# Four homes for the experts' weights, bank pairs by kind in a first pass, and values cast on two engines in turn

## The reference, cut to what matters

```python
x = x + xattn0(layernorm(x), ctx)      # 16 heads of 16, softmax over 12544 keys, then a small MLP
x = x + attn0(layernorm(x))            # causal, 16 heads of 16
x = x + experts0(layernorm(x))         # top 2 of 8: gelu(x @ W1[e] + b1[e]) @ W2[e] + b2[e], W1 256 x 1024
x = x + xattn1(layernorm(x), ctx)      # 16 heads of 64, softmax over 12544 keys
x = x + attn1(layernorm(x))
x = x + experts1(layernorm(x))         # top 2 of 8, silu gated
# xattn: q = x @ Wq; k = ctx @ Wk; v = ctx @ Wv; softmax(q k^T * scale) v @ Wo
```

## Time and profile before

| | before |
|---|---|
| median of 3 runs | 1709.82 us (1706.11 to 1713.38) |
| profiled execution | 1709.02 us, span 1707.3 us |
| TensorE busy | 1469.4 us, 86% |
| VectorE busy | 1085.0 us, 64% |
| ScalarE busy | 1095.1 us, 64% |
| granted TensorE clock, mean | 0.959 of full speed |

### The profile page before, as it was taken

One profiled execution on the slowest core, in us unless ns is written; L12 is line 12 of the kernel. 1 busy time (PEld: TensorE's weight loads), 2 busy tenths in 40 slices (PEclk: granted clock), 3 DMA queues, 4 the chain that ended last, 5 costly groups with the idle time before them and its releaser, 6 DMA issues.

```text
span 1707.3 us, 37451 instructions
## 1 busy us (share of the span) xinstructions
PE 1469.4 (86%) x15312; PEld 989.3 (58%) x15312; DVE 1085.0 (64%) x1663; ACT 1095.1 (64%) x1612; POOL 91.0 (5%) x90
## 2 busy tenths in 40 slices
PE   4777776999997698978898976999999899999959
PEld 2333334777775486434444434777777677777748
DVE  4687775111112303667777778888888888888842
ACT  4998985777773134756766664767677676776721
POOL 5211110000000003100000000000000000000000
PEclk8999998999998699999999997999999999999979
DMA  3232216434332055554444434777777577788530
GB/s 125 84 113 76 88 64 176 88 67 90 76 67 99 0 198 176 167 179 151 149 149 149 151 141 96 138 136 135 138 136 136 107 137 136 137 219 163 143 111 4
DMA packets 122415, 209.00 MB, mean 122 GB/s; under 512 B 8236, under 2 KB 113158, under 8 KB 122246
## 3 DMA queue, kind: packets, MB, share of 16 engines
q1 hardware_dynamic: 122246, 206.60, 47.5%
HBM read 142.22 MB, written 64.36 MB: 121 GB/s over the span
## 4 chain that ended last, share of the span: by engine, by line
PE 45%; DVE 21%; ACT 16%; issue 15%; DMA 3%; SPq 0%; DVEq 0%; POOL 0%; ACTq 0%; POOLq 0%
PE ps L590 44%; ACT ps L966 7%; DVE W L1140 6%; DVE v L1140 4%; DVE v L1252 4%; DVE small L1204 3%; ACT p L1003 2%; ACT p L991 2%; ACT W L989 1%; DMA W<-in_L_ffn_W_dram 1%; ACT W L991 1%; DMA keys_hi<-p 1%; DVE W L1170 1%; ACT stage L976 1%; ACT p L966 1%
## 5 line engine op out<-in xcount | busy, mean ns | idle before, releaser
L966 ACT ACTIVATE p<-ps 128x512 f16<-128x512 f32 (+1 forms) x490 | 327.7, 679 | 195.6 <-PE ps L590 193.0
L1140 DVE TENSOR_TENSOR p<-ps,p 128x512 f16<-128x512 f32 (+1 forms) x467 | 351.5, 753 | 127.8 <-ACT p L991 65.6
L590 PE MATMUL ps<-W,q_all 128*32 128x128 f32 (+2 forms) x2268 | 220.2, 303 | 58.2 <-DVE W L1170 33.1
L590 PEld LDWEIGHTS ps<-q_all,W 128*128 128x128 f16 (+1 forms) x3544 | 232.6, 99 | 57.2 <-issue 6.7
L590 PE MATMUL ps<-q_all,W 128*128 128x128 f16 (+2 forms) x3544 | 263.1, 227 | 0.9 <-DVE q_all L1136 0.7
L966 ACT ACTIVATE ps<-ps 128x512 f32<-128x512 f32 x392 | 233.7, 596 | 0.0
L590 PEld LDWEIGHTS ps<-W,q_all 128*32 128x32 f32 (+2 forms) x2268 | 110.1, 110 | 152.3 <-DVE W L1170 44.9
L590 PE MATMUL ps<-wv,ctxT_a_hi 128*128 128x512 f16 (+1 forms) x588 | 157.6, 350 | 33.0 <-DVE v L1140 32.7
L590 PE MATMUL ps<-v,p 128*128 128x130 f16 x3136 | 169.7, 207 | 5.1 <-DVE p L1140 5.1
L1243 DVE COPY q_all<-ps 128x256 f32<-128x256 f32 x98 | 37.0, 420 | 206.4 <-PE ps L590 206.3
L1003 ACT CAST p<-ps 128x896 f16<-128x896 f32 x180 | 151.0, 934 | 14.1 <-PE ps L590 13.8
(11 more groups left out here) (218 smaller groups left out, 1710.0 us busy)
## 6 DMA issues: line engine op xcount, KB each, us to landing
W<-keys_hi SPq DMA_DIRECT2D x56, 896.0 KB, 14.4
W<-keys_low SPq DMA_DIRECT2D x28, 896.0 KB, 11.4
keys_hi<-p SPq DMA_DIRECT2D x75, 224.0 KB, 1.9
keys_low<-p SPq DMA_DIRECT2D x75, 224.0 KB, 1.9
keys_hi<-W SPq DMA_DIRECT2D x65, 224.0 KB, 1.9
keys_low<-W SPq DMA_DIRECT2D x65, 224.0 KB, 1.9
W<-in_L_ffn_W_dram SPq DMA_DIRECT2D x10, 1024.0 KB, 8.4
W<-in_ctx_dram SPq DMA_DIRECT2D x14, 672.0 KB, 4.4
```

The source lines that it names most:

```text
L590: return pe.matmul(out_, lhsT, rhs, start=start, stop=stop, **kw)
L966: return act.activation(out_, in_, ACT.Exp, scale=scale)
L1140: return dve.tensor_tensor(out_, a, b, op)
```

## The change

Three things change.

Experts: `EXPERT0` gives each expert two half homes, and there are four whole ones; the fourth is made of a part of `W` and of `p16`, which attention 0 uses up to its last tile. Every expert has its own load semaphore. Expert 3 is asked for once attention 0 has weighed its last tile, 4 after one down product, 5 after two, 6 after four, 7 after five. Wq and Wk follow expert 7, Wv and Wo the last down product.

First pass: a function `pairs_of` gives each turn its pair and the turn that last used it. For the first attention that is the same as before. For the second, keys turns alternate between pairs 0 and 1 and max turns between pairs 2 and 3.

Tile loop: for odd tiles ScalarE casts the values ahead of its exponentials, and VectorE only subtracts.

```diff
+        def pairs_of(turns, apart):
+            pairs, before, count, last = [], [], {"keys": 0, "max": 0}, {}
+            for i, (kind, n, h) in enumerate(turns):
+                if apart:
+                    pair = count[kind] % 2 + (0 if kind == "keys" else 2)
+                    count[kind] += 1
+                else:
+                    pair = i % 4
+                pairs.append(pair)
+                before.append(last.get(pair))
+                last[pair] = i
+            return pairs, before
+
+        (PAIR0, BEFORE0), (PAIR1, BEFORE1) = pairs_of(TURNS[0], False), pairs_of(TURNS[1], True)
+        PAIR, BEFORE = (PAIR0, PAIR1), (BEFORE0, BEFORE1)
...
-        EXPERT0 = (stage[:, 0:4096], W[:, 11200:15296], W[:, 0:4096])
+        E0_STAGE = stage[:, 0:2048], stage[:, 2048:4096]
+        E0_EARLY = W[:, 11200:13248], W[:, 13248:15296]
+        E0_KEYS = W[:, 0:2048], W[:, 2048:4096]
+        E0_PROBS = W[:, 4096:6144], p16_flat.bitcast(F32)
+        EXPERT0 = (E0_STAGE, E0_EARLY, E0_KEYS, E0_PROBS, E0_STAGE, E0_EARLY, E0_PROBS, E0_STAGE)
...
-            for e in range(1, NE + 1):
-                if e + 2 < NE:
-                    sp.wait_ge(exp_summed, e)
-                    load_expert0(e + 2)
-                elif e + 2 == NE:
-                    sp.wait_ge(exp_summed, e)
-                    load_blocks(ld_w, L1.wq, d["L1_xattn_Wq"])
-                    load_split(ld_w, L1.wk, d["L1_xattn_Wk"])
-                elif e + 1 == NE:
-                    sp.wait_ge(exp_summed, e)
-                    load_split(ld_wv, L1.wv, d["L1_xattn_Wv"])
-                    load_blocks(ld_w2, L1.wo, d["L1_xattn_Wo"])
+            sp.wait_ge(weighed, NT)
+            load_expert0(3)
+            sp.wait_ge(exp_summed, 1)
+            load_expert0(4)
+            sp.wait_ge(exp_summed, 2)
+            load_expert0(5)
+            sp.wait_ge(exp_summed, 4)
+            load_expert0(6)
+            sp.wait_ge(exp_summed, 5)
+            load_expert0(7)
+            load_blocks(ld_w, L1.wq, d["L1_xattn_Wq"])
+            load_split(ld_w, L1.wk, d["L1_xattn_Wk"])
+            sp.wait_ge(exp_summed, NE)
+            load_split(ld_wv, L1.wv, d["L1_xattn_Wv"])
+            load_blocks(ld_w2, L1.wo, d["L1_xattn_Wo"])
...
             def first_pass(L):
                 for i, (kind, n, h) in enumerate(TURNS[L.n]):
-                    for left in turn_left(L, i - 4):
+                    slot = PAIR[L.n][i]
+                    for left in turn_left(L, BEFORE[L.n][i]):
                         pe.wait_ge(*left)
...
                     for t in range(NT):
                         i = g * NT + t
+                        if i % 2:
+                            act.wait_ge(values_summed, V0N + i + 1)
+                            if i >= 2:
+                                act.wait_ge(weighed, NT + i - 1)
+                            act.copy(v_tile(i)[:, :, 0:L1.dh],
+                                     ps[:, V1_BANK, 0:L1.gw].rearrange("p (h c) -> p h c", h=8)).then_inc(values_hi, 1)
                         for j in range(2):
...
             def split_values1(i):
...
-                dve.tensor_copy(v4[:, :, 0:L1.dh], vp).then_inc(values_hi, 1)
+                if i % 2 == 0:
+                    dve.wait_ge(values_summed, V0N + i + 1)
+                    if i >= 2:
+                        dve.wait_ge(weighed, NT + i - 1)
+                    dve.tensor_copy(v4[:, :, 0:L1.dh], vp).then_inc(values_hi, 1)
                 dve.wait_ge(values_hi, i + 1)
```

More of the change, by code:

```diff
@@ L110, in perceiver_kernel @@
         ld_x, ld_bias, ld_w, ld_w2, st_out = (sem(n) for n in ("ld_x", "ld_bias", "ld_w", "ld_w2", "st_out"))
-        ld_exp = [sem(f"ld_exp{n}") for n in range(3)]
+        ld_exp0 = [sem(f"ld_exp0_{e}") for e in range(NE)]
         ld_exp1 = [sem(f"ld_exp1_{e}") for e in range(NE)]
@@ L121, in perceiver_kernel @@
         REST_IN = (3 * 16, 4 * 16)
-        def exp0_in(e):
-            return 32 * (e // 3 + 1)
         dve_own, pool_own = sem("dve_own"), sem("pool_own")
@@ L257, in turn_left @@
         def turn_left(L, i):
-            if i < 0:
+            if i is None:
                 return []
@@ L410, in load_expert0 @@
             def load_expert0(e):
-                region = EXPERT0[e % 3]
-                load_blocks(ld_exp[e % 3], region[:, 0:2048], d["L0_ffn_W1"][e])
-                load_blocks(ld_exp[e % 3], region[:, 2048:4096], d["L0_ffn_W2"][e])
+                load_blocks(ld_exp0[e], EXPERT0[e][0], d["L0_ffn_W1"][e])
+                load_blocks(ld_exp0[e], EXPERT0[e][1], d["L0_ffn_W2"][e])
             wait_stores(L0, NCH - 1)
@@ L654, in first_pass @@
                 for i, (kind, n, h) in enumerate(TURNS[L.n]):
-                    for left in turn_left(L, i - 4):
+                    slot = PAIR[L.n][i]
+                    for left in turn_left(L, BEFORE[L.n][i]):
                         pe.wait_ge(*left)
-                    if i == 3:
+                    if slot == 3 and BEFORE[L.n][i] is None:
                         pe.wait_ge(q_low, 4) if L is L1 else pe.wait_ge(q_hi, 2)
                     if kind == "ab":
-                        turn_ab(n, i % 4)
+                        turn_ab(n, slot)
                     elif kind == "lo":
-                        turn_lo(n, i % 4)
+                        turn_lo(n, slot)
                     elif kind == "keys":
@@ L666, in first_pass @@
                             project_q(L0)
-                        project_keys(L, n, i % 4)
+                        project_keys(L, n, slot)
                     else:
@@ L670, in first_pass @@
                             pe.wait_ge(q_hi, h // L.hp + 1 if L is L0 else 4)
-                        score_maxima(L, n, h, i % 4)
+                        score_maxima(L, n, h, slot)
                 pe.wait_ge(shift_made, L.n + 1)
@@ L866, in hidden0 @@
                 b = e % 2
-                w1 = by_rows(EXPERT0[e % 3][:, 0:2048], 2, F0)
-                pe.wait_ge(ld_exp[e % 3], exp0_in(e))
+                w1 = by_rows(EXPERT0[e][0], 2, F0)
+                pe.wait_ge(ld_exp0[e], 32)
                 if e >= 2:
@@ L880, in down0 @@
                 b = e % 2
-                w2 = by_rows(EXPERT0[e % 3][:, 2048:4096], NF, D)
+                w2 = by_rows(EXPERT0[e][1], NF, D)
                 pe.wait_ge(hid_made, 2 * (e + 1))
@@ L1013, in first_pass @@
                     elif kind == "keys":
-                        keys_out(L, n, i % 4)
+                        keys_out(L, n, PAIR[L.n][i])
                     elif kind == "max" and not is_direct(L, n, h):
-                        copy_maxima(L, n, h, i % 4)
+                        copy_maxima(L, n, h, PAIR[L.n][i])
             def attend0():
@@ L1200, in first_pass @@
                     elif kind == "keys":
-                        keys_low_out(L, n, i % 4)
+                        keys_low_out(L, n, PAIR[L.n][i])
                     elif kind == "max" and is_direct(L, n, h):
                         dve.wait_ge(max_scored, n_max(L, n, h))
-                        dve.tensor_reduce(mpart[:, h, n // 4:n // 4 + 1], ps[:, i % 4 * 2:i % 4 * 2 + 2, 0:MAXC], AX.XY,
+                        dve.tensor_reduce(mpart[:, h, n // 4:n // 4 + 1], ps[:, 2 * PAIR[L.n][i]:2 * PAIR[L.n][i] + 2, 0:MAXC], AX.XY,
                                           ALU.max).then_inc(max_reduced, 1)
@@ L1248, in split_values1 @@
                 vp = ps[:, V1_BANK, 0:L1.gw].rearrange("p (h c) -> p h c", h=8)
-                dve.wait_ge(values_summed, V0N + i + 1)
-                if i >= 2:
-                    dve.wait_ge(weighed, NT + i - 1)
-                dve.tensor_copy(v4[:, :, 0:L1.dh], vp).then_inc(values_hi, 1)
+                if i % 2 == 0:
[3 more added lines that the diff above has]
+                    dve.tensor_copy(v4[:, :, 0:L1.dh], vp).then_inc(values_hi, 1)
                 dve.wait_ge(values_hi, i + 1)
```

## The result

The changed kernel takes 1727.4 us (median of four), and its ratio to the kernel before is 1.0096 (1.0073 to 1.012): 16 us slower (12 to 21), where 19 were forecast. Its profiled execution has a span of 1724.2 us, 16.9 more than the 1707.3 of before. Three moments cut the two spans into comparable parts: the start of expert 1's hidden product, the end of the last down product, and the first step of VectorE's final maximum tree, which follows the first pass.

The account below looks back on a forecast made before the run. Loads among the experts and latencies around loops in the first pass and tile loop bound the kernel; experts -5, bank pairs +19 and casts +5 gave +19 us, forecast 1729 us, range 1709 to 1744.

Parts of the forecast that it names:

- Experts, -5: First layer's experts: earlier weight loads remove most TensorE stops, gaining 2.3 to 5.8 us, taken as 5.
- The covers: Experts' weight loads: those of 3, 4 and 5 hidden behind earlier work; TensorE waits 0.9 to 2.4 us at expert 6.
- its 0 to 1.5: Ahead of expert 7: TensorE waits 0 to 1.5 us more for the weights.
- the 0.2 and 0.5 us: Expert 7's share in what the experts still pay: 0.2 us at best, 0.5 at worst.
- The slower clock, 1.7 us at worst: Among the experts: at worst products behind the remaining stop run at the slow clock again, costing 1.7 us.
- Bank pairs, +19: Second attention's first pass: two more matmuls behind each direct reduction, 0.38 us per pair of blocks, together +19, bounds 10 and 24.
- The count of pairs: First pass: of 56 pairs of blocks, 47 to 49 lengthen by 0.38 us, giving 18 to 18.6 us.
- The upper bound's ground: First pass: TensorE's longer pauses might cost the clock as much as three 2.36 us stops did, making it +24.
- The rival that these matmuls would fall into lost time: First pass: the product's extra wait falls into time TensorE loses anyway, bank pairs cost 0, whole 1710 us; chance 13%.
- the rival that own pairs would free the keys: First pass: TensorE waits for the keys' pair, so separate pairs save 47 us, whole 1663 us; chance 5%.
- the rival's own condition: First pass: next product's pair must be drained before TensorE reaches it, 4.6 or 5.0 us after the key projection's start.
- Casts, +5: Tile loop: only one of two equal loops is shortened, and ScalarE's cast delays exponentials 0.05 us in 98 tiles; bounds 0 and 15.

Follow-up runs that it names:

- the reduction went first: Changed kernel, with VectorE reducing a block's direct product ahead of the next block's low keys and the merges in the second attention's first pass: 1668.8 us, ratio 0.9749.
- even tiles: Changed kernel, with ScalarE casting the values of the even tiles in place of the odd ones: ratio 1.0069.
- all tiles: Changed kernel, with ScalarE casting the values of every tile and VectorE's cast removed: 1696.2 us, ratio 0.991.
- both measurements: Kernel before, with only ScalarE's casts of the odd tiles added, measured twice: ratios 1.0004 and 0.9996.
- the runs with a faster loop: Changed kernel with ScalarE casting every tile's values, 1696.2 us; also with the reduction ahead of the low keys, 1634.9; then with late expert weights loaded one at a time, 1626.9.

## Why the prediction held

**Experts, -5.** Measured -5.8 as a whole and 5.1 in the trace. The covers came out as worked: none for experts 3, 4 and 5, and 1.60 us at expert 6, between the 0.9 and 2.4. Expert 7 had the stop of expert 6 as extra cover and waited for nothing, the lower end of its 0 to 1.5; the 0.2 and 0.5 us that the sum gave it come from no row. The slower clock, 1.7 us at worst, didn't come.

**Bank pairs, +19.** Measured 21 alone; from the last down product to the maximum tree 21.3. The step itself, two more matmuls of 0.191 us behind each direct reduction, is to be seen in the links of 14 and 12. The count of pairs held too: between one direct reduction and the next, 46 steps of the changed kernel's pass are longer by 0.37 to 0.38 us, 17.3 together, where 47 to 49 were counted. The term was a little too small for what stands beside these steps. The first chunk's grow by 0.8 us in all, where 0.6 was forecast; one step, behind a stop of TensorE of over 6 us that both kernels have (at 732.58 in the changed one, with products at half rate behind it), by 1.5; and from the last reduction to the maximum tree it is 1.2 us more. The last two weren't in the sum. The upper bound's ground, that TensorE's longer pauses would cost the clock, isn't seen in the loop: from 745 to 1025 us the changed kernel was granted 1.00. The rival that these matmuls would fall into lost time is refuted by the same links, and the rival that own pairs would free the keys by the run with the bank pairs alone. Where they do pay, after the reduction went first, is as the rival's own condition says: the product's pair has to be drained before TensorE is back at it.

**Casts, +5.** The mechanism was right, both in that only one of two loops was cut (even tiles, all tiles) and in that ScalarE's cast pushes the exponentials. They start 1.77 us after the value products (1084.78 to 1086.55), where it was 1.73 before (1055.46 to 1057.19), and the period rose by 0.04 where 0.05 was forecast. The term's effect on the whole was mis-sized: 3.7 us in the loop's steady part, less what the loop's first tiles and the scattered stops take out of it again; in the whole it measures 0 (-2.7 to +2.7 over both measurements). The rule of the Trainium skill ("Perfetto Trace Analysis", Optimizing Scalar/DVE Operations) that offloading work to ScalarE may make sense where VectorE is saturated isn't borne out for this change: VectorE's busy share in the loop fell by 11 points, from 89% to 78%, and nothing was won. It is true of the step beyond, in which no cast is left in the loop.

**The sum.** 19 forecast, 16.4 measured (12 to 21). Alone, the experts gave 0.8 us more than forecast, the pairs cost 2.4 more and the casts 5 less, so the misses of the pairs and of the casts partly cancel. The forecasts of the experts and of the pairs lie within the intervals of their measurements, that of the casts doesn't.

## What to carry to other kernels

Count what follows the releasing instruction. A ring of buffers over mixed work isn't just a number of slots: it decides which later instruction each drain releases, and a split by kind can hand the late drain to an earlier instruction, here two matmuls earlier in a loop that some 50 pairs of blocks go round. When a loop runs through two alternating copies, relieving one gains nothing until the other is relieved too. Before buffers are moved, look at the order in which the draining engine takes its work: one reordering of VectorE's instructions was worth 59 us, the new buffers then 12, and a faster loop afterwards had to have its transfers spread, since one that was hidden came out.

## What was unexpected

In the second group of tiles above all, TensorE has single stops with nothing in the profile to release it: 1.57 us in the changed kernel, 2.69 us with the bank pairs alone, and 3.2 to 3.5 us in the runs with a faster loop. They make much of the scatter between profiles of that stretch, and their cause wasn't found. And TensorE's clock answered a stop of 5.85 us by running the next group of 16 matmuls in 1.87 us and not 1.06, at a granted clock of 0.50, the lower of its two levels (1.2 and 2.4 GHz), while the stop of 1.60 us among the experts left the next products at full rate (3.84 us, granted 1.00).
